# Silu on one engine, a ninth D unit per pass, and a planner that knows table loads and the lag at an image's border

## What is computed

```python
x = x + conv3x3(gn(x))                         # layer 0
x = x + L1(gn(x)); x = x + L2(gn(x)); x = x + L3(gn(x))

def mamba(x):                                  # in L1, for 4 orders of tokens/channels
    u, z = split(x @ in_proj_w.T)
    uc = silu(causal_conv4(u) + conv_b)
    dtr, B, C = split(uc @ x_proj_w.T)
    dt = softplus(dtr @ dt_proj_w.T + dt_proj_b)
    h[t] = exp(dt[t] * A) * h[t-1] + (dt[t] * uc[t]) * B[t]      # 256 x 16 states
    y[t] = h[t] . C[t]
    return ((y + uc * D) * silu(z)) @ out_proj_w.T
```

## Time and profile before

| | us |
|---|---|
| median of 3 executions | 15722.11 |
| lowest and highest | 15718.98, 15722.39 |
| the profiled execution | 15723.84 |
| its span, first to last instruction | 15722.0 |

### The profile page before, as it was taken

The page is one execution under the profiler, slowest core; times in us unless marked ns, Lnnn a source line. Parts: engine busy times, 40 slices in busy tenths (PEclk is TensorE's granted clock), DMA queues, the critical chain, the costliest instruction groups (busy, mean ns, idle before and its releaser), DMA issues.

```text
span 15722.0 us, 186855 instructions
## 1 busy us (share of the span) xinstructions
PE 12802.9 (81%) x58652; PEld 8108.3 (52%) x58652; DVE 13720.0 (87%) x10423; ACT 8801.8 (56%) x10272; POOL 14797.4 (94%) x4747
## 2 busy tenths in 40 slices
PE   6888888888888888888888888888888888888886
PEld 3555555555555555555555555555555555555554
DVE  6888888889888898888888888988889888888886
ACT  4555555555555555555555555555555555555553
POOL 6999999999999999999999999999999999999996
PEclk8888888888888888888888888888888888888886
DMA  4655555555555555555555555555555555555553
GB/s 165 225 215 216 210 214 220 213 214 216 212 221 214 213 218 212 218 216 212 218 212 216 219 215 212 217 211 221 217 212 218 211 218 217 213 218 211 218 220 131
DMA packets 619399, 3336.26 MB, mean 212 GB/s; under 512 B 69973, under 2 KB 69984, under 8 KB 355944
## 3 DMA queue, kind: packets, MB, share of 16 engines
q1 hardware_dynamic: 618216, 3321.93, 56.8%
HBM read 3241.95 MB, written 29.36 MB: 208 GB/s over the span
## 4 chain that ended last, share of the span: by engine, by line
POOL 38%; issue 27%; PE 17%; DVE 13%; ACT 4%; DVEq 0%; POOLq 0%; ACTq 0%; DMA 0%; SPq 0%
POOL ring L868 21%; POOL ring L851 14%; PE work L1391 9%; DVE ring L1379 7%; PE y_acc L1406 6%; DVE slot L1368 3%; POOL du L812 2%; PE slot L1391 2%; PE y_acc L1391 1%; ACT ring L1024 1%; ACT L884 1%; DVE u_conv L1164 0%; PE work L1406 0%; ACT slot L1024 0%; ACT L987 0%
## 5 line engine op out<-in xcount | busy, mean ns | idle before, releaser
L868 POOL TENSOR_TENSOR ring<-ring,c_rows 128x2048 f32<-128x2048 f32 x2048 | 9281.3, 4533 | 583.2 <-DVE ring L1379 581.8
L1406 PE MATMUL y_acc<-wk,ring 128*128 128x128 f32 x32768 | 5117.6, 311 | 981.2 <-POOL ring L868 831.0
L1406 PEld LDWEIGHTS y_acc<-wk,ring 128*128 128x128 f32 x32768 | 4531.1, 163 | 2377.0 <-POOL ring L868 1213.6
L1379 DVE TENSOR_TENSOR_SCAN ring<-slot,ring 128x1024 f32<-128x1024 f32 x2048 | 4666.8, 2279 | 613.1 <-POOL ring L851 587.0
L1379 DVE TENSOR_TENSOR_SCAN ring<-ring,slot 128x1024 f32<-128x1024 f32 x2048 | 4679.2, 2285 | 201.4 <-DVE slot L1368 14.2
L851 POOL TENSOR_TENSOR ring<-du,b_rows 128x1024 f32<-128x1024 f32 x2048 | 4838.4, 2363 | 14.2 <-POOL du L812 14.1
L1024 ACT ACTIVATE slot<-dt,a_neg 128x1024 f32<-128x1024 f32 x2048 | 2283.6, 1115 | 3071.3 <-DVE ring L1379 3063.3
L1368 DVE TENSOR_TENSOR slot<-du,slot 128x1024 f32<-128x1024 f32 x2048 | 2487.4, 1215 | 471.2 <-PE slot L1391 440.0
L1024 ACT ACTIVATE ring<-dt,a_neg 128x1024 f32<-128x1024 f32 x2048 | 2328.6, 1137 | 22.4 <-issue 10.6
L1391 PE MATMUL work<-h_new,fused 128*128 128x512 f32 x4096 | 2292.6, 689 | 0.0
L1391 PE MATMUL slot<-stack,sel 96*128 96x512 bf16 x4096 | 1462.5, 444 | 953.6 <-DVE ring L1379 940.7
(11 more groups left out here) (186 smaller groups left out, 10011.4 us busy)
## 6 DMA issues: line engine op xcount, KB each, us to landing
c_rows<-cb_rows_scratch SPq DMA_DIRECT2D x2048, 1024.0 KB, 4.6
b_rows<-cb_rows_scratch SPq DMA_DIRECT2D x2048, 512.0 KB, 5.4
x_next<-in_x SPq DMA_DIRECT2D x32, 512.0 KB, 5.4
x_new<-x_next SPq DMA_DIRECT2D x32, 512.0 KB, 6.7
h_old<-h_new SPq DMA_DIRECT2D x32, 512.0 KB, 6.6
x_old<-x_new SPq DMA_DIRECT2D x32, 512.0 KB, 6.8
out<-x_old SPq DMA_DIRECT2D x32, 512.0 KB, 6.6
cb_rows_scratch<-stack SPq DMA_DIRECT2D x128, 96.0 KB
```

Source lines behind the costliest of these rows:

```text
L868: pool.tensor_tensor(pair, pair, c_rows[:, k % CB_BUFS, :, :], ALU.mult).then_inc(prod_ready, 1)
L1379: dve.tensor_tensor_scan(slot, a, b, 0.0, MUL, ADD).then_inc(scan_done, 1)
L1406: ins = pe.matmul(chunk(out_t, j), chunk(x, j), kc("ident"), is_transpose=True, start=start and j % (BANK // P) == 0, stop=stop, skip_grou ...
```

## The change

Four things change.

- KIND of the last unit of a pass is D: nine inputs of a pass are formed on DVE, seven on POOL.
- Silu is one activation of ACT, with the convolution's bias as its bias operand; the halved weights, the bias matmul and DVE's silu_u and silu_z are gone. silu_pair lets PE fill both banks of work (conv_in or z of both halves), and then ACT runs the two Silus.
- Table sets: natural_log_exp_and_others is home (decay, dt_exp, dt_ln); Silu, Tanh and Sin are in silu_and_others, Gelu in its own. A load comes where a step or a decay needs it, not after the step.
- lay() counts 1.3 us for a change of table, prefers steps of a foreign table while it is loaded, lets a stream hold both banks, and starts PE 11 us and POOL 9.5 us late in images other than the first; plans are compared by the latest engine less its lag. Some costs in SIDE_COST change. hold() waits once per engine.

The diff, cut to its core (left out: setup steps z_half and bias, tiles and arguments of the bias, and the scale of fused, now 1.0):

```diff
--- before.py
+++ after.py
@@ -45,7 +45,7 @@
 UNITS = PASSES * NST
 RING = 8
 PAIRS = UNITS // 2
-KIND = "DPDPDPDPDPDPDPDP"
+KIND = "DPDPDPDPDPDPDPDD"
 N_D, N_P = PASSES * KIND.count("D"), PASSES * KIND.count("P")
 CB_BUFS = 4
@@ -99,7 +99,10 @@
 
 
 
-OTHER_TABLES = ("q_sin", "squeeze_gelu", "silu2", "mlp_gelu", "sine")
+HOME = "natural_log_exp_and_others"
+TABLE = {**dict.fromkeys(("silu", "silu2", "gate_tanh", "xa_tanh", "sine", "q_sin"), "silu_and_others"),
+         **dict.fromkeys(("squeeze_gelu", "mlp_gelu"), "gelu_and_others"),
+         **dict.fromkeys(("decay", "dt_exp", "dt_ln", "dtexp2", "dtln2", "decay2", "a_exp", "a_exp2"), HOME)}
 
 
@@ -129,23 +132,25 @@
     return s
 
 
-def silu(of, d, h, c):
-
-    b = (of, d, h, c)
-    return [step(("silu_tanh", d, h, c, of), "A", b), step(("silu_" + of, d, h, c), "D", b)]
+def silu_pair(of, d, h, name, parts, after=()):
+
+    key = lambda c: (of, d, h, c)
+    steps = []
+    for c in range(2):
+        for k in parts:
+            steps += [step((name, d, h, *k, c), "P", key(c), after if not steps else [])]
+    return steps + [step(("silu", of, d, h, c), "A", key(c)) for c in range(2)]
 
 
 def operands(d, first=False):
 
     steps = []
     for h in range(HALVES):
-        for c in range(2):
-            steps += [step(("conv_in", d, h, k, c), "P", ("u", d, h, c)) for k in range(TAPS)] + silu("u", d, h, c)
+        steps += silu_pair("u", d, h, "conv_in", [(k,) for k in range(TAPS)])
     if d % 2:
         for h in range(HALVES):
-            for c in range(2):
-                taken = [] if c or first and d == 1 else [("take", 2 + h if d == 3 else "before")]
-                steps += [step(("z", d, h, c), "P", ("z", d, h, c), taken)] + silu("z", d, h, c)
+            taken = [] if first and d == 1 else [("take", 2 + h if d == 3 else "before")]
+            steps += silu_pair("z", d, h, "z", [()], taken)
     for c in range(2):
         b = ("xproj", d, c)
...
@@ -267,18 +271,21 @@
 SIDE_COST = {"conv_in": .9, "xproj": .9, "z": 1., "dt_proj": .95, "mix": .9, "conv0": .9, "nin": 1., "adjust": .9,
              "turn_y": .5, "rest": .3, "dtproj2": .9, "in2": 2., "spread2": .95, "mask2": 1.25, "xproj2": .9, "out2": .9, "unitary": .5,
              "post": 1.8, "group_mean": .7, "angles": 1.8, "gates": .5, "mlp1": .5, "mlp2": .5, "turn": .3, "squeeze": .3,
-             "silu_tanh": .6, "silu_u": .75, "silu_z": .7, "dt_cb_rows": .6, "part": .6, "dt_abs": .7, "dt_relu": .7,
+             "silu": .68, "dt_cb_rows": .6, "part": .6, "dt_abs": .7, "dt_relu": .7,
              "dt_exp": 1.06, "dt_ln": .9, "dt_sum": .7, "dt_u": 2.4, "turned_y": .6, "h1": .8, "relu2": .8,
-             "squeeze_gelu": 3., "silu2": 3.2, "mlp_gelu": 1.6, "sine": 2.9, "decay2": .6, "stats": .7, "norm": 1.25,
+             "squeeze_gelu": .4, "silu2": .8, "mlp_gelu": .3, "sine": .6, "decay2": .6, "stats": .7, "norm": 1.25,
              "add0": .75, "add1": .7, "rows": 1.2, "cols": 1.9, "taps2": 1.7, "tapsum2": 1.05, "dta2": 1.1, "input2": .7,
              "scan2": 1.25, "prod2": .7, "ysum2": 1.05, "outer_h": 1.25, "outer_w": 1.25, "times_x": .7, "add2": .7,
              "result": .75, "group_rstd": .55, "take": 1.2, "du2": .7, "dterm2": .7, "dadd2": .7, "yz2": .7}
 UNIT_COST = {"b": 1.26, "scan": 2.32, "spread": .5, "sum": .9, "decay": 1.13, "prod": 4.55, "input": 2.38}
 DUE = {"b": 0., "scan": .4, "spread": -1., "decay": -1.5, "prod": 1.2, "input": -1., "sum": 4.}
-HOP, STEP_DELAY, SOON = .12, .9, .2
+TABLE_LOAD = 1.3
+HOP, STEP_DELAY = .12, .9
+SOON = .2
 ROWS_IN = 12.
 SUM_LATER = 4
 LOAD_AT, KEEP_H_AT, OUT_AT, KEEP_X_AT, MOVE_AT = 6, 16, 48, 50, 58
+LAG = {"P": 11., "A": 0., "D": 0., "G": 9.5}
 PACES = [3.2 + .05 * i for i in range(36)]
@@ -389,8 +396,10 @@
         by[("take", p)] = p * NST + NST + 4
     by[("turned_y", "this", 1, 0, 1)] = UNITS - 4
     want = deadlines(streams, by, pace)
-    end, free, at = {}, dict.fromkeys("PADG", 0.), dict.fromkeys("PADG", 0)
-    banks, held, kept, used = [0., 0.], {}, [None, None], {}
+    end, free, at = {}, dict(dict.fromkeys("PADG", 0.) if kind == "first" else LAG), dict.fromkeys("PADG", 0)
+    banks, kept, table = [0., 0.], [None, None], HOME
+    held = [{} for _ in streams]
+    final = [{x[2]: k for k, x in enumerate(stream)} for stream in streams]
     heads, plan = [0] * len(streams), []
 
     def ready(names):
@@ -399,9 +408,13 @@
     def side_ready(i):
         name, e, bank, after = streams[i][heads[i]]
         t = ready([(x, 0) for x in after] + ([(streams[i][heads[i] - 1][0], 0)] if heads[i] else []))
-        if bank is not None and held.get(i) != bank:
+        if bank is not None and bank not in held[i]:
             return max(t, min(banks) + HOP)
         return t
+
+    def table_of(e, i):
+        name = programs[e][at[e]][0] if i < 0 else streams[i][heads[i]][0]
+        return TABLE.get(name[0], table) if e == "A" else table
 
     while True:
         best = None
@@ -416,33 +429,40 @@
             if not choices:
                 continue
             soon = min(x[0] for x in choices) + SOON
-            choice = min((x for x in choices if x[0] <= soon), key=lambda x: x[1])
+            choices = [x for x in choices if x[0] <= soon]
+            if table != HOME and e == "A":
+                choices = [x for x in choices if x[2] >= 0 and streams[x[2]][heads[x[2]]][0][0] in TABLE
+                           and table_of(e, x[2]) == table] or choices
+            choice = min(choices, key=lambda x: x[1])
             if best is None or choice[0] < best[0]:
                 best = (choice[0], choice[2], e)
         if best is None:
             break
         t, i, e = best
+        change = TABLE_LOAD * (table_of(e, i) != table)
+        table = table_of(e, i)
         if i < 0:
             op, place = programs[e][at[e]]
             at[e] += 1
-            end[op] = free[e] = t + unit_cost(op)
+            end[op] = free[e] = t + unit_cost(op) + change
             continue
         name, _, bank, after = streams[i][heads[i]]
         place = programs[e][at[e]][1] if at[e] < len(programs[e]) else END[e]
         waits = list(after) + ([streams[i][heads[i] - 1][0]] if heads[i] else ["start"])
-        if bank is not None and held.get(i) != bank:
+        if bank is not None and bank not in held[i]:
             w = banks.index(min(banks))
             waits += [kept[w] or "start"]
-            held[i], used[i], banks[w] = bank, w, 1e9
-        plan.append((place, name, e, used.get(i, 0), waits))
+            held[i][bank], banks[w] = w, 1e9
+        plan.append((place, name, e, held[i].get(bank, 0), waits))
         heads[i] += 1
-        free[e] = t + SIDE_COST.get(name[0], .3)
+        free[e] = t + SIDE_COST.get(name[0], .3) + change
         end[name] = free[e] + (.1 if e == "P" else 0.)
-        if bank is not None and (heads[i] == len(streams[i]) or streams[i][heads[i]][2] != bank):
-            banks[used[i]], kept[used[i]], held[i] = end[name], name, None
+        if bank is not None and heads[i] == final[i][bank] + 1:
+            w = held[i].pop(bank)
+            banks[w], kept[w] = end[name], name
     if any(heads[i] < len(x) for i, x in enumerate(streams)) or any(at[e] < len(programs[e]) for e in "PADG"):
         return None, 1e9
-    return plan, max(end.values())
+    return plan, max(free[e] - LAG[e] for e in LAG)
...
@@ -686,13 +704,17 @@
 
         def hold(eng, e, base, of, names):
 
+            need = {}
             for name in names:
                 if name == "start":
                     for other in "ADG":
                         if not (isinstance(base[other], int) and base[other] == 0):
-                            eng.wait_ge(side[other], base[other])
+                            need[other] = max(need.get(other, 0), 0)
                 elif name in of and not (e == "P" and of[name][0] == "P"):
-                    eng.wait_ge(*done(base, of[name]))
+                    other, n = of[name]
+                    need[other] = max(need.get(other, 0), n)
+            for other, n in need.items():
+                eng.wait_ge(*done(base, (other, n)))
 
         def lane_of(name):
...
             def ready_table(name):
-                if name[0] in ("silu_tanh", "gate_tanh", "xa_tanh"):
-                    want("exp_and_others")
-                elif name[0] in ("dt_ln", "dtln2"):
-                    want("natural_log_exp_and_others")
+                if name[0] in TABLE:
+                    want(TABLE[name[0]])
 
             def step(name, s, w):
                 k = name[0]
@@ -909,9 +927,12 @@
                 elif k == "h1":
                     c = name[1]
                     ins = act.activation(half(h_mid, c), w, ACT.Relu, bias=bnw[:, 0, 4:5], scale=bnw[:, 0, 2:3])
-                elif k == "silu_tanh":
-                    _, d, h, c, of = name
-                    ins = act.activation(half(u_conv[:, d % 2, h, :] if of == "u" else silu_z[:, h, :], c), w, ACT.Tanh)
```

(17 more changed lines are left out.)

48 lines of the change are left out of this document (13 added, 35 removed).

## The result

The changed kernel takes 15342.47 us (median of 4, 15333.09 to 15352.46) against 15722.25 (median of 4): a ratio of 0.9758, 95% interval 0.9741 to 0.9775. That is 380 us faster, where 794 were forecast. The time lies in rival B's interval, 15070 to 15370; whether B's reason is right is what the experiments are about.

What follows compares the result with a forecast made beforehand. POOL was taken to set the pace wherever DVE has little beside its units. Sum: 15722 - 594 (a) - 242 (d) - 8 (e) + 48 (f) = 14926, 14928 with what lies around the span; range 14720 to 15260 us.

Steps and rivals of the forecast that it cites:

- rival B: Whole kernel: DVE and PE become the bound together, (f) from +6 to +15.5 us per image, 15070 to 15370; chance 0.20.
- two homes of its waits: POOL's waits for scans: the image's border, 7.8 us, and a dense stretch of 110 us where POOL and DVE idle some 11.5.
- (a): Unit 15 of each pass becomes a D unit: POOL loses 256 inputs at 2.32 us, 594 us saved.
- (b): Silu by ACT alone, taken at 0.60 us each: DVE loses 768 steps, 13.9 us per image.
- (c): ACT's table loads: at most 36 per image instead of 31.8, 5.4 us more, on ACT's idle time.
- Rival E: Slower: ACT's visits delay the decays every time, 2.5 us, 30 per image, 15838 us; chance 0.04.
- (d): Image border: PE's spread of unit 2 ahead of side steps removes POOL's 7.8 us idling at 31 borders, 242 us saved.
- nothing is late next: At the border, once the spread of unit 2 comes earlier, POOL waits for no other step, so all 7.8 us are gained.
- (e): Prologue and tail: ten small DVE steps go, 4 us, and paired conv_in halves save 4.7 us; together 8 us saved.
- (f): Idle time that comes or goes, valued from the dense stretch's busy times: +1.5 us per image, 48 us added.
- The two-bank rule: Under (f): a pair holds one bank of work while waiting for the other, and other streams do with fewer; no separate size.

Runs made afterwards that it cites:

- the thin Silu steps: b_kind_thin and b_thin: DVE's silu_u and silu_z on 32 of 512 columns, against b_kind and the kernel before: 15891.19 and 15765.57 us.
- h_nokind: a_halves with KIND as in the kernel before, eight D units per pass: 15331.98 us, ratio 0.9744.
- a_halves: The changed kernel with silu pairs turned into halves, each half's Silu behind its own conv_in, one bank at a time: 14976.96 us, ratio 0.9528.
- h_best: a_halves with two planner numbers changed, SOON 0.08 instead of 0.2 and POOL's lag 7 instead of 9.5 us: 14894.21 us, ratio 0.9474.
- b_kind_thin: b_kind in the same written order, with DVE's silu_u and silu_z on 32 of 512 columns: 15891.19 us, ratio 1.0106.
- b_kind: The kernel before with KIND of unit 15 made D and nothing else: 15966.03 us, ratio 1.0157.
- h_hold: a_halves with one planner edit: a pair's first bank is given back only with the pair's last Silu: 15402.22 us, ratio 0.9795.
- b_thin: The kernel before, eight D units, same written order, with DVE's silu_u and silu_z on 32 of 512 columns: 15765.57 us, ratio 1.0029.

## Why the prediction was right or wrong, point by point

**What bounds the kernel.** Right in naming POOL and two homes of its waits. Wrong in reading the second as two engines at their capacity. Busy shares near 90% on both looked like load; the thin Silu steps showed that taking some 350 us of busy time from DVE gives 75 us, or none, and nothing in the dense passes.

**(a) Unit 15.** POOL's busy time fell by 576 us against 594 forecast, and the five quiet passes kept nearly all of their gain. In the whole, beside halves, the ninth unit is worth 355 us, and 239 are given back: 594 is the term for a kernel whose other waits don't grow. Of the 18.6 us per image, the profiled executions of h_nokind and a_halves show 3.6 of 7.0 in passes 3 to 5 and 8.6 of 11.6 in the other five. Most of the loss is in pass 4, which takes 61.5 us with nine D units and 58.2 with eight.

**(b) Silu.** Silu of z takes 597 ns, as tanh. Silu of u, with its bias, takes 688 and not 595:

```profile
L933 ACT ACTIVATE u_conv<-work,wk 128x512 f32<-128x512 f32 x512 | 352.4, 688 | 234.3 <-PE work L1389 224.3
...
L935 ACT ACTIVATE silu_z<-work 128x512 f32<-128x512 f32 x256 | 152.9, 597 | 12.3 <-PE work L1389 6.9
```

That is 16 x 0.09 = 1.5 us per image on an idle engine. A row of the kernel before had the nearer price, an activation of the same size from the same bank that also takes a bias per channel: `L935 ACT ACTIVATE dt<-work,wk 128x512 f32<-128x512 f32 x512`, 684 ns. DVE's busy time ended at 13567, forecast some 13500.

**(c) Table loads.** At most 36 per image were forecast, and 1144 / 32 = 35.8 came. Their delay of decays was nothing (19.3 us of DVE's waits; 23.6 before). In a_halves, with 56.6 loads per image and ACT busy for 66%, they wait 89.9 us, 2.8 per image, and the kernel is the faster one. Rival E, slower by ACT's visits, never came near.

**(d) The border.** The stall fell from 7.8 to 2.7 us, 158 us over 31 borders instead of 242, and moved from the product of units 2 and 3 to that of 0 and 1. The step that failed is "nothing is late next": DVE's take was queued ahead of scan 1, and the prediction followed PE and POOL only.

**(e) Prologue.** The first dt_u on POOL starts at 134.98 instead of 144.33: 9.3 us, 8 forecast.

**(f) Idle time.** This is the term that failed. +48 us were put down; without it the sum is 14878, and 15342 - 14878 = 464. Of that 84 are the border's rest (d) and some 380, 12 us per image, are waits in passes 3 to 5: with POOL's 7.0 us less these were due at 182.5, and took 194.6 (means). One bank at a time brings them to 181.4. The prediction did name the two-bank rule, in one sentence under (f), and gave it no price of its own. It took the dense stretch's balance of busy times for the price of everything, and busy times say nothing of how long a bank is held. A lower bound was in the rows: a pair holds its first bank for the whole of the second half's conv_in, and one half took 5.43 us even in the serial prologue. The hold traced above was some 31 us, since the second half first had to get the other bank from back's chain. And the planner had a price: by its own estimate, which knows the bank rule, pairs cost 6.5 us per image more than halves, 206 us of the 366. With halves the sum of the prediction is nearly the chip's: (f) is then 14977 - 14878 = 99 us, 71 of them the border's rest of 2.3 us.

**The rivals.** B's interval held the time, and half of its text, "with two-bank holds in an in-order queue", was the cause; its headline, that DVE and PE become the bound together, wasn't. That the time fell into B's interval is half luck, since most of B's case was the balance of busy times. Its chance of 0.20 was too low: a step with two banks, twelve times per image, deserved more, since PE's order was already the cause of the border's stall.

## What to carry to other kernels

When a change makes a step hold a shared buffer (here one of two PSUM banks) while it waits for more work on the same buffer, price the holding time, not the busy time: count who else goes through that buffer in the stretch where waits already are. Saving an instruction on an engine that idles (ACT's table loads) is no reason for such a hold. Where an order is computed by a planner, its own estimate of both variants is a first price. And one edit's effect can't be read from one order: run a second order of each kernel, since the luck of an order was as large as the parts in question, and compare stretch by stretch, since a gain in one and a loss in another can cancel in the whole time.

## What the runs showed of the hardware

Two orders of the same instructions differ by 180 us (15722 and 15902) and in PE's mean granted clock, 0.850 and 0.839 (shares of 2.4 GHz, means of stretches at 2.4 and at 1.2). Over the kernels the clock tends to be higher where the time is shorter, 0.851 in the changed kernel, 0.869 in a_halves, 0.884 in h_best (14894), but not in step with it: b_kind_thin has 0.830 at 15891 us and b_kind 0.843 at 15966, h_hold 0.861 at 15402.

In pass 3 the changed kernel's PE got 0.70 and was busy for 55.2 us with 213 matmul records; before, it got 0.74 and was busy for 51.1 us with as many. With halves it got 0.86 in pass 3 and did 247 in 54.7 us. On average over the middle images, PE is busy for 164.1 us of passes 3 to 5 with pairs (clock 0.832), 162.8 with the longer hold (0.823) and 156.9 with halves (0.866). So up to 7 of the 13 us between pairs and halves may pass through the clock. Whether the lower clock is a cause of the longer passes or comes of PE's pauses in them, no run here tells apart.

And 356 us less work on DVE made one order slower by 0.3% (b_thin); whether by the clock, 0.837 against 0.850, or by an earlier release that met a worse moment in another queue, was not told apart.
